# Rows combined at 64 columns before the projection, gathers tied to transposes, one hand-written grid for all engines

## What is computed

```python
e = stack([tbl_f[ids[:, f]] for f in range(26)], axis=1)     # 512 x 26 rows of 64
x = layer_norm(dense @ Wd.T, gd, bd)                         # 512 x 128
y = layer_norm(einsum('bnd,ed->bne', e, Ws), gs, bs)         # each row 64 -> 128, normalised
y = einsum('bne,pn->bep', y, Wsi)                            # 26 rows combined into 32
y = layer_norm(y, gsi, bsi)                                  # over the 32
T = concatenate([x[:, None], swapaxes(y, 1, 2)], axis=1)     # 33 x 128 for each sample
Z = einsum('bnd,bmd->bnm', T, T)                             # Gram matrix, 528 entries kept
z = layer_norm(Z[tril] @ Wl.T, gl, bl)                       # 512, 384 kept
h = relu(concatenate([z, dense], 1) @ W_top1 + b1)           # 640 -> 512
h = relu(h @ W_top2 + b2)                                    # 512 -> 256
out = h @ W_top3                                             # 256 -> 1
```

## Time and profile before

| | |
|---|---|
| median of 3 runs | 320.21 us (318.27 to 320.65) |
| span of the profiled execution | 318.9 us |
| PE busy | 184.9 us (58%) |
| DVE busy | 119.3 us (37%) |
| ACT busy | 111.7 us (35%) |
| POOL busy | 101.2 us (32%) |
| mean granted TensorE clock, share of 2.4 GHz | 0.775 |
| longest item of the chain that ended last | another core or an unknown queue, 35% |

### The profile page before, as it was taken

The page is one execution under the profiler, slowest core; times in us unless marked ns, Lnnn a source line. Parts: engine busy times, 40 slices in busy tenths (PEclk is TensorE's granted clock), DMA queues, the critical chain, the costliest instruction groups (busy, mean ns, idle before and its releaser), DMA issues.

```text
span 318.9 us, 4779 instructions
## 1 busy us (share of the span) xinstructions
PE 184.9 (58%) x1794; PEld 132.2 (41%) x1794; DVE 119.3 (37%) x356; ACT 111.7 (35%) x478; POOL 101.2 (32%) x118
## 2 busy tenths in 40 slices
PE   0566340001111100000799999999999989998976
PEld 0444220001010000000566776567875678756756
DVE  3542210210000000000484888575576655776520
ACT  1133110100000000000745887376674667744332
POOL 4787777777777777710000000000000000000000
PEclk9956575555555555555579999999999999999998
DMA  4841111111111111100000011001200002010000
GB/s 162 271 166 25 27 32 25 25 29 25 28 26 25 29 25 25 28 8 0 0 2 0 2 40 31 1 2 23 45 3 2 2 20 44 8 22 14 2 0 0
DMA packets 14861, 9.91 MB, mean 31 GB/s; under 512 B 12099, under 2 KB 12501, under 8 KB 14582
## 3 DMA queue, kind: packets, MB, share of 16 engines
q1 hardware_dynamic: 11078, 5.22, 6.0%
q0 software_dynamic: 3328, 3.41, 5.6%
q10 hardware_dynamic: 432, 0.97, 0.9%
HBM read 7.76 MB, written 0.00 MB: 24 GB/s over the span
## 4 chain that ended last, share of the span: by engine, by line
PE 41%; another core or an unknown queue 35%; ACT 9%; DVE 6%; issue 3%; DMA 2%; POOL 2%
PE py L387 10%; PE tu L371 5%; PE pf L437 5%; PE pz L402 4%; PE pf L418 4%; ACT junk L576 2%; PE py L384 2%; ACT ysq L584 2%; PE tu L365 2%; PE pf L447 2%; DVE proj L811 2%; POOL emb L337 2%; ACT u_sd L580 1%; ACT zT L615 1%
## 5 line engine op out<-in xcount | busy, mean ns | idle before, releaser
L337 POOL DMA_INDIRECT emb<-tables_dram,rows_at x104 | 99.0, 952 | 31.6 <-issue 31.4
L818 DVE TENSOR_REDUCE y_ms<-ysq 128x16 f32<-128x512 f32 x32 | 21.9, 684 | 134.3 <-ACT ysq L584 117.2
L371 PE MATMUL tu<-proj_w,embT 128*128 128x256 f32 x104 | 36.4, 433 | 60.5 <-ACT embT L570 43.1
L387 PE MATMUL py<-wbd,proj 128*128 128x192 f32 (+4 forms) x256 | 58.3, 339 | 22.4 <-issue 22.4
L387 PEld LDWEIGHTS py<-wbd,proj 128*128 128x128 f32 x256 | 44.0, 212 | 36.1 <-issue 35.2
L371 PEld LDWEIGHTS tu<-proj_w,embT 128*128 128x128 f32 x104 | 19.3, 212 | 65.0 <-ACT embT L570 44.1
L594 ACT ACTIVATE gram<-pz 64x272 f32<-64x272 f32 x32 | 12.1, 379 | 85.8 <-remote 85.6
L402 PE MATMUL pz<-T 128*32 128x34 f32 x1024 | 25.8, 200 | 27.8 <-issue 26.1
L402 PEld LDWEIGHTS pz<-T 128*32 128x32 f32 x1024 | 21.1, 114 | 39.7 <-issue 37.1
L576 ACT ACTIVATE junk<-tu 128x128 f32<-128x128 f32 x104 | 27.4, 272 | 22.3 <-remote 12.4
L811 DVE SCALAR_TENSOR_TENSOR proj<-tu,u_r,comb_w 128x128 f32<-128x128 f32 x104 | 31.7, 347 | 1.8
(11 more groups left out here) (127 smaller groups left out, 174.0 us busy)
## 6 DMA issues: line engine op xcount, KB each, us to landing
emb<-tables_dram,rows_at POOLq DMA_INDIRECT x104
w<-w_dram SPq DMA_DIRECT2D x1, 1280.0 KB
wl<-wl_dram SPq DMA_DIRECT2D x1, 1024.0 KB
zn<-gram SPq DMA_DIRECT2D x24, 32.0 KB, 1.9
zr<-gram SPq DMA_DIRECT2D x24, 32.0 KB, 1.9
denseT<-denseT_dram ACTq DMA_DIRECT2D x1, 512.0 KB
w<-w_dram SPq DMA_DIRECT2D x1, 512.0 KB
comb_w<-comb_w_dram ACTq DMA_DIRECT2D x1, 311.0 KB, 3.2
```

Of the source, the lines that this page charges most:

```text
L337: pool.indirect_dma_start(emb[:, k, :], None, t["tables"], bass.IndirectOffsetOnAxis(ap=rows_at[:, k // HALF, k % HALF:k % HALF + 1], axis=0),
L371: pe.matmul(TU[(PAIRS * g + j) % NTU][:, P:P + 2 * E], embT[:, j, :], proj_w[:, P:], start=True, stop=True).then_inc(u_done, 1)
L387: mm = pe.matmul(PY[(QUARTERS * g + q) % NPY][:, :, :].rearrange("p b c -> p (b c)")[:, col:col + n], proj[:, j, tile % 2, :], wbd[:, :, : ...
L818: dve.tensor_reduce(y_ms[:, q, :], ysq[:, q % 2, :, :], AX_X, ALU.add).then_inc(y_ms_ready, 1)
```

## The change

1. Quads. The row-wise stages work on four tiles (two pairs, 26 quads in all). `transposes(i)` makes two transposes; one ACT copy of 256 columns follows. The variance of a projected row is no longer taken from the projected row: `spread_products` multiplies the transposed rows with a 64x64 matrix (`mbd`, twice on a diagonal, 128 columns), and DVE multiplies the result with the row itself and sums (`u_sums`). DVE then scales the 64 columns of the gathered row in place (`scale_rows`).
2. Combine first, project after. `combine` takes the scaled rows as its stationary side, two tiles side by side (the host puts the ids in another order, so that both tiles of a pair have the same weight slice). A block of 32 samples (`BLOCKS` = 4 in a group) fills a bank; ACT copies it (`c_copy`); `project` makes, for each half of the block, one bias matmul and one float32 matmul with 64 rows and 512 moving columns.
3. Gram products of two samples in one matmul: 64 weight columns, 67 moving columns, 8 where there were 16.
4. Gathers: POOL waits, before each quad from the fourth on, for the transposes of the quad three before it.
5. All engines follow a grid of ticks, four to a pair, with one offset for each stage, up to tick 190; what is left is written call by call.
6. Stacking: 16 DMAs a group as before, with all four quarters of the Gram matrices; for the last group no DMAs but copies on POOL, DVE and ACT.
7. At the start PE runs the dense projection and its transposes before the first `transposes(0)`, and builds `mbd` (one transpose and one matmul with an ACT copy after each).

```diff
-            gather(range(HALF))
+            def gather(pairs):
+                for pair in pairs:
+                    g, j = divmod(pair, PAIRS)
+                    if pair % 2 == 0:
+                        wait_if_any(pool, t_done, pair // 2 + 1 - QUADS_AHEAD)
+                    for half in range(2):
+                        pool.indirect_dma_start(...).then_inc(gathered[pair], 16)
+            gather(range(6))
...
-            gather(range(HALF, NG * TILES))
+            gather(range(6, STEPS))
```

```diff
+            def spread_products(i):
+                pe.wait_ge(embT_ready, i + 1)
+                for half in range(2):
+                    mm = pe.matmul(TU[i % NTU][:, QUAD + P * half:QUAD + P * half + P],
+                                   embT[:, i % 2, P * half:P * half + P], mbd[:, :], start=True, stop=True)
+                mm.then_inc(v_done, 1)
+            def combine(step):
+                g, j = divmod(step, PAIRS)
+                pe.wait_ge(scaled, (g * PAIRS + j) // 2 + 1)
+                of = emb[:, 2 * (g * PAIRS + j):2 * (g * PAIRS + j) + 2, :].rearrange("p t d -> p (t d)")
+                for c, col, n, at in pieces(j):
+                    ...
+                    mm = pe.matmul(PC[m % NPC][...][:, col:col + n], of, wbd[...][:, at:at + n], ...)
+            def project(m):
+                pe.wait_ge(cs_ready, m + 1)
+                wait_if_any(pe, T_ready, 2 * m)
+                for half in range(2):
+                    pe.matmul(PY[half], bias_l[at, :], bias_r[at, :, :], ...)
+                for half in range(2):
+                    mm = pe.matmul(PY[half], wg[at, :], cs[at, m % 2, :, :], ...)
+                mm.then_inc(y_done, 1)
+            def gram_products(m, half):
+                wait_if_any(pe, gram_ready, 2 * m + half)
+                for b in range(SLOTS):
+                    for h in range(2):
+                        of = T[:, at + 2 * b + h, :]
+                        mm = pe.matmul(PZ[2 * PR * h:2 * PR * h + 2 * PR, ITEMS * b:ITEMS * (b + 1)],
+                                       of[:, 0:2 * PR], of, start=True, stop=True)
```

```diff
+            def u_sums(i):
+                dve.wait_ge(v_done, i + 1)
+                dve.tensor_tensor(prod[:, i % 2, :], TU[i % NTU][:, QUAD:2 * QUAD], emb[...], ALU.mult)
+                dve.tensor_reduce(u_sum[:, i % 2, :], prod[...], AX_X, ALU.add)
+                dve.tensor_scalar(u_ms[:, i % 2, :], u_sum[:, i % 2, :], 0.0, EPS, ALU.max, ALU.add)
+            def scale_rows(i):
+                dve.wait_ge(u_sd_ready, i + 1)
+                dve.reciprocal(u_r[:, i % 2, :], u_sd[:, i % 2, :])
+                rows = emb[:, 4 * i:4 * i + 4, :]
+                dve.tensor_tensor(rows, rows, u_r[...].to_broadcast([P, 4, D]), ALU.mult).then_inc(scaled, 1)
```

The grid on PE, cut to the stages that the text speaks of (tick 8 is one quad; a block's offset counts from its last pair):

```diff
-            for step in range(STEPS):
-                ...
+            for tick in range(END):
+                for m in blocks_at(tick, 16):
+                    gram_products(m, 0)
+                for i in quads_at(tick, -8):
+                    spread_products(i)
+                for m in blocks_at(tick, 4):
+                    project(m)
+                for step in pairs_at(tick, 1):
+                    combine(step)
+                for m in blocks_at(tick, 19):
+                    gram_products(m, 1)
+                for i in quads_at(tick, -13):
+                    transposes(i)
+                ...
```

More of the change, by code:

```diff
@@ L359, in _ @@
         def _(pe):
[L360 to L372, removed]
@@ new lines, in _ @@
+            last = NG - 1
+            end = BLOCKS * NG - 1
+            flat_layer(last - 1, 0)
+            combine(STEPS - 4)
+            spread_products(QUADS - 1)
+            combine(STEPS - 3)
+            flat_layer(last - 1, 1)
+            project(end - 1)
+            flat_layer(last - 1, 2)
+            flat_layer(last - 1, 3)
+            combine(STEPS - 2)
+            combine(STEPS - 1)
+            gram_products(end - 2, 0)
+            flat_layer(last - 1, 4)
+            gram_products(end - 2, 1)
@@ new lines, in _ @@
+            project(end)
+            gram_products(end - 1, 0)
+            mlp1_dense(last, 0)
+            z_transposes(last - 1)
+            gram_products(end - 1, 1)
+            mlp1(last - 1, 0)
+            gram_products(end, 0)
+            mlp1_dense(last, 1)
+            gram_products(end, 1)
+            mlp1(last - 1, 1)
+            mlp1(last - 1, 2)
+            mlp1_dense(last, 2)
+            mlp1(last - 1, 3)
+            for k in range(5):
+                flat_layer(last, k)
@@ L555, in _ @@
+            mlp1_dense(last, 3)
             mlp2(last - 1)
+            z_transposes(last)
             mlp3(last - 1)
-            z_transposes(last)
-            mlp1(last, (0, 1, 2, 3), (0, 1, 2))
+            for k in range(4):
+                mlp1_rest(last, k)
             mlp2(last)
@@ new lines, in y_square, with y_spread, gram_copy @@
+            def y_square(m):
+                act.wait_ge(y_done, m + 1)
+                for half in range(2):
+                    act.activation(ysq[:, half, :, :], PY[half][:, :, :], ACT.Square,
+                                   scale=float(PR) ** -0.5).then_inc(ysq_ready, 1)
+            def y_spread(m):
+                act.wait_ge(y_ms_ready, 2 * m + 2)
+                act.activation(y_sd[:, m % 2, :, :], y_ms[:, m % 2, :, :], ACT.Sqrt, bias=eps[:, :]).then_inc(y_sd_ready, 1)
+            def gram_copy(m, half):
+                g, q = m // BLOCKS, 2 * (m % BLOCKS) + half
+                act.wait_ge(z_done, 2 * m + half + 1)
@@ L725, in _ @@
-            late_stack(last, slice(EARLY, NZ))
+            y_spread(end)
+            gram_copy(end - 1, 1)
+            gram_copy(end, 0)
             x_sums_copy(last)
+            gram_copy(end, 1)
+            late_stack(last, slice(EARLY, NB))
             h1_relu(last - 1)
@@ L922, in _ @@
+            last = NG - 1
+            end = BLOCKS * NG - 1
+            u_sums(QUADS - 1)
+            scale_rows(QUADS - 1)
+            linear_features(last - 1, 3)
+            y_sums(end - 1)
+            normalise(end - 1)
+            z_stats(last - 1)
+            z_normalised(last - 1)
+            y_sums(end)
+            normalise(end)
+            late_stack(last, slice(EARLY, NB))
             merge(last)
-            linear_features(last)
+            for k in range(4):
+                linear_features(last, k)
```

777 lines of the change are left out of this document (416 added, 361 removed).

## The result

The changed kernel takes 238.34 us (median of 5 runs, 235.97 to 244.36); the kernel before takes 318.27 us beside it (median of 5, 317.88 to 320.65). The ratio is 0.744, with a 95% interval of 0.7395 to 0.7485; ratios with an interval are taken over the runs near the fastest of each kernel, so they are not quite the quotient of the medians. The profile after is of an execution of 240.35 us (span 238.5), 2.0 us over the median.

A forecast was written before the change was run, and what follows sets the result against it. Late word of PE's work during gathers was taken to bound the kernel up to 150.66 us, PE after it. Start 24, 25 quads of 7.9, tail 40.7 and 1.3 us gave 263 us, range 206 to 301.

The forecast's parts named there:

- The mechanism: Word of finished PE instructions gets out late while gathers run (0.21 to 1.40 us each); the tie's pauses release it.
- The quad: Each of 25 quads: 5.0 us of gathers plus a 2.9 us pause for 56 instructions' words, 7.9 us.
- under 3 us from the transposes' end to ACT's copy: Sign of the tie's effect: ACT copies the transposed rows under 3 us after the transposes end.
- The arithmetic gains nothing: PE's own time for a quad stays 5.8 us as before, its changes summing to -0.3 to +0.3 us.
- The start: Time until transposes(0), now behind the transposes of x_rows on PE: 24 us (20 to 28).
- The tail: From the last transposes to the end: same work in finer order, 40.7 us kept, within 4 either way.
- The sum: Start, quads and tail: 24 + 25 x 7.9 + 40.7 = 262.2 us; with 1.3 us from span to median, 263.
- Full overlap: Rival: with gathers in runs of four the lag disappears, PE bounds a quad at 5.8 us; 211 us, chance 0.22.
- The tie changes little: Rival: even in runs of four a word takes 1.40 us, a quad 8.9 us; 289 us, chance 0.12.
- The lag on the chain: Rival: gathers and PE's work don't overlap at all, a quad takes 10.8 us; 336 us, chance 0.13.
- The ports: Rival: each scale_rows on DVE holds up a gather by 0.61 us, a quad takes 8.5 us; 279 us, chance 0.05.
- Faster, 0.85: Chance that the changed kernel is faster by over 1%: 0.85, against same 0.02 and slower 0.13.

The follow-up runs named there:

- e12: Changed kernel with e10's later merge, and the gathers' wait on the transposes taken out: 299.95 us, ratio 0.9462 to the kernel before.
- e10: Changed kernel with merge and the first flat_layer product six ticks later, in the tail behind the next two combinations: 240.53 us, ratio 0.7533 to the kernel before.
- e5: Changed kernel unaltered, in a session where the kernel before takes 195.78 us: 198.16 us.
- e8: Kernel before, unaltered, run once more for its trace: 197.85 us, with 195.96 us for the kernel before beside it.
- e11: e10 with the first transposes and their copy also ahead of the dense part's: 237.76 us, ratio 0.7491 to the kernel before.

## Why the prediction came out as it did

Predicted were 263 us, with 206 to 301 as the range; measured 238.34, inside the range and 1.7 us below the forecast's own 240 to 280. The quads were 21.5 us too long in the sum and the start 6.8; that the tail was 4.5 too short hid a part of it, which is luck.

**The mechanism** held: the tie breaks the run of gathers, and the words get out in the pauses. e12 against e10 shows by one edit that the tie gains. The paces that the forecast rests on were seen again: 1.40 us in an old run (e12); early in the run of eight, 12 instructions between two words to ACT in 58.62 - 55.77 = 2.85 us, 0.24 each; after its end 16 in 0.36 us, from the word of the Gram passes (62.99) to that of the transposes behind them (POOL at 63.35).

**The quad** was the term that was mis-sized, 7.9 us for 7.04, 21.5 us over 25 quads. I added the pause to the gathers as 2.9 us, by a fixed count of words still owed. The trace has 42.1 + 7.5 us of POOL's waits (for PE, and remote) over the 23 quads that can wait, 2.2 us each; 5.0 + 2.2 is 7.2, and the last quads, whose gathers are already made, go faster (5.0 us from the last but one to the last, 188.10 to 193.13). The shape was wrong too: I had runs of four and pauses of 2 to 4 us; there are also eights and a twelve, with pauses from 1.2 to 8.1 us. PE works off its quads in bunches: the transposes of two quads start 1.9 us apart (50.77 and 52.65), and then POOL has leave for eight gathers. The sign "under 3 us from the transposes' end to ACT's copy" held from 117 to 158 us, where all runs are of four (0.8 to 2.7 us in six quads), and failed beside the longer runs, where it went up to 6.7 us (58.18 to 64.90).

PE's own time, which I held unchanged at 5.8 us a quad, was too large as well, though this hid behind the gathers. In the clean sessions PE is busy for 155.0 us in the changed kernel (page of e5) and 172.5 in the kernel before (e8), 17.5 us less, and the quad takes 5.40 us with the stalls at the merges in it. "The arithmetic gains nothing" is wrong for PE's work.

**The start** was 17.2 us where I took 24 (20 to 28), 6.8 us less. I left `x_rows` at the time it has in the kernel before, 22.19 us. There the dense part's matmuls stand behind the first transposes; in the changed kernel they stand ahead of them, and `x_rows` starts at 15.6:

```profile
L904 DVE TENSOR_TENSOR x_rows<-pf,x_r x1: 691/691/691, 15.6 to 15.6; 128x512 f32<-128x512 f32 x1
```

**The tail** was 45.2 us where I took 40.7. The prediction looked at the transfers of the last group alone and kept the rest as "the same work, in finer order". The order is what counts: the merge of the third group, asked for before its transfers have landed, falls into the tail:

```profile
195.64 0.01 DVE L997 LOAD_MASK_SELECT zm<-z  x1 [5.47 <-DMA z<-gram]
...
198.62 2.04 PE L492 MATMUL pf<-wl,zm 128*128 128x512 f32 x2 [4.72 <-ACT y_row L762]
```

To take PE's 4.72 us off would give 40.5, but the runs with the merge later don't reach that: their tails are 43.3 (e10), 42.1 (e11: 231.3 - 189.2) and 41.7 us (e12: 297.7 - 256.0). So the order makes up 1.9 to 3.5 of the 4.5 us, and the rest stays open. The order of the list on DVE was in the diff (`merge` at tick 27), and so was the length of the transfers in the trace before; I hadn't set the one against the other.

**The sum** then closes: 262.2 - 21.5 - 6.8 + 4.5 = 238.4, the span being 238.5. It must, since the three parts are cut from that one span; between its execution (240.35 us) and the median lie 2.0 us more.

**The rivals.** Full overlap (211 us) is false for the late sessions: a quad of 7.04 us is not PE's 5.8. In the clean sessions it is what happens, 5.40 us a quad, and the kernel before does it as well. The tie changes little (289 us): refuted by e12, in which it changes 59 us. The lag on the chain (336 us): gathers and PE's work did overlap, since the quad is well under its 10.2 us. The ports (279 us): the 20 gathers that overlap a `scale_rows` take 0.960 us in the mean and the other 84 take 0.957, so nothing near 0.61 us was added. I had also misread the rows of before: more than two gathers overlap a placing there, and those at 26.00 and 27.24 us take 0.94. The one of 1.55 us at 16.45 comes again in e8 (16.42), so it isn't chance; what lengthens it isn't shown.
Of the Trainium skill's rule in "SBUF — State Buffer", "Who interferes with whom", by which a DMA that looks stalled by the Vector engine is one whose descriptors GpSimd makes, no run here shows an effect of `scale_rows`; single gathers of 1.5 us stand in every trace, with `scale_rows` and without.

**Faster, 0.85**, was right of the runs that were to be predicted, and right for a reason that belongs to their session. Where words are not late, the changed kernel gains nothing and may be 1% or so slower. That the lateness might come and go was in no rival of mine; I had read it as fixed, from one trace and three runs that agreed.

## What to carry to other kernels

Where an engine starts long after its input was finished and nothing in the trace fits the end of the wait, compare the kernel with itself in another session before you explain the design by it: here the same kernel takes 318 or 196 us. If gathers from GpSimd run beside a chain of short TensorE instructions, tie them to their consumer: in the changed kernel that is worth 59 us where the words are late, and in both kernels it was free where they are not. In a hand-written order, a merge that waits for a row of transfers belongs behind them in time (the end of the last issue plus about 1.3 us here), since all that its engine owes to others is queued behind it.

## What the hardware did that I had not expected

- The same program, 318.27 and 195.8 us. Both are on record under one chip number: 195.79 us in the first session and 317.67 in the last. With no late words, the gathers themselves go as ever (944 to 947 ns), so the difference isn't in their issue. What sets it off stays open; no experiment here could bring it about.
- Where words are late, they come at 1.40 us for each TensorE instruction, weight loads counted, whether TensorE is working or has stopped (e12). The engine's own waits for ACT and DVE are not slowed: in e12 ACT ends a copy at 102.92 us (102.54 and 0.38) and TensorE starts on it at 102.97.
- The stacking transfers are of 32 KB each and start 0.68 us apart, and the merge starts 1.3 us after SP has ended the issue of the last (75.66 to 76.94, and 151.86 to 153.14 in e5); from the start of that issue, at 151.3, it is 1.8 us. For a DMA issued from GpSimd the Trainium skill ("DMA: Bandwidth & Descriptors", "Anatomy of one DMA — SWDGE (gpsimd) path") gives a fixed cost of some 2 us, most of it the completion and not the transfer. The gathers' 2.5 us from issue to landing (median of e5 and of e8) are of that size; how much of it is completion no view here shows.
